# Other due times for the last element's normalisation pieces, squares and transpositions

## The reference

```
x = x + xattn(layernorm(x), ctx, ctx)
    # t = Wt v, p = Wp q, g = Wg k; att = sum over a group of p * g, 8 groups
    # y = Wz (att * t), group by group; group norm of y, times gn_w plus gn_b, plus v
x = x + ffn(layernorm(x))
    # t = x[:, perm] as 16 heads of 128; gelu(t up[h]) down[h]; back to the old order
```

## Time and profile before

| | us |
|---|---|
| median of 3 runs | 1515.17 (1512.41 to 1517.02) |
| profiled execution, its own time | 1520.61 |
| its span, first to last instruction | 1518.8 |
| PE busy | 1496.8 (99%) |
| DVE busy | 1201.1 (79%) |
| ACT busy | 1065.3 (70%) |
| POOL busy | 967.8 (64%) |

### The profile page before, as it was taken

The page is one execution under the profiler, slowest core; times in us unless marked ns, Lnnn a source line. Parts: engine busy times, 40 slices in busy tenths (PEclk is TensorE's granted clock), DMA queues, the critical chain, the costliest instruction groups (busy, mean ns, idle before and its releaser), DMA issues.

```text
span 1518.8 us, 19146 instructions
## 1 busy us (share of the span) xinstructions
PE 1496.8 (99%) x6592; PEld 1231.6 (81%) x6592; DVE 1201.1 (79%) x1514; ACT 1065.3 (70%) x1321; POOL 967.8 (64%) x765
## 2 busy tenths in 40 slices
PE   8999999999999999999999999999999999999998
PEld 7878887887878888888888888888888888877786
DVE  4999868887778767887778877887678876889786
ACT  4636757855778568784687847877478783899786
POOL 1673685298862668525794357835589264888787
PEclk9999999999999999999999999999999999999999
DMA  9998797786667937778376774767748676758886
GB/s 330 329 375 332 230 312 281 270 267 210 226 238 267 286 110 223 253 256 266 125 250 243 250 248 140 266 240 249 215 151 281 250 235 186 259 193 261 272 275 223
DMA packets 166865, 374.76 MB, mean 247 GB/s; under 512 B 14960, under 2 KB 80496, under 8 KB 158576
## 3 DMA queue, kind: packets, MB, share of 16 engines
q1 hardware_dynamic: 141424, 281.25, 56.3%
q0 software_dynamic: 25344, 92.29, 17.1%
HBM read 287.45 MB, written 86.03 MB: 246 GB/s over the span
## 4 chain that ended last, share of the span: by engine, by line
PE 69%; POOL 7%; DVE 7%; DMA 6%; ACT 5%; issue 4%; SPq 1%; POOLq 0%; ACTq 0%; DVEq 0%
PE PP L965 11%; PE PP L950 11%; PE PP L904 11%; PE PP L969 6%; PE PP L953 5%; PE PP L908 5%; PE PP L891 5%; PE PP L892 5%; PE PP L886 5%; PE PP L921 3%; PE PP L925 2%; DVE R L1096 2%; DMA WW<-w_scratch 1%; ACT Z L1043 1%; DMA FB<-xg_scratch,perm_sb 1%
## 5 line engine op out<-in xcount | busy, mean ns | idle before, releaser
L950 PE MATMUL PP<-GG,WW 128*128 128x512 f32 x1008 | 270.0, 390 | 1.0 <-DMA WW<-w_scratch 1.0
L1058 ACT ACTIVATE PP<-PP 128x1024 f32<-128x1024 f32 x256 | 262.1, 1024 | 0.0
L1261 DVE TENSOR_TENSOR R<-PP,R 128x1024 fp32r<-128x1024 f32 x175 | 213.6, 1220 | 55.0 <-ACT PP L1058 54.6
L904 PE MATMUL PP<-R,WC 128*128 128x512 f32 x1024 | 253.2, 389 | 0.2 <-ACT Z L1010 0.2
L1342 POOL TENSOR_TENSOR X<-X,RAW 128x512 f32<-128x512 f32 x112 | 192.5, 1753 | 95.3 <-DVE bn L1081 68.8
L1057 ACT ACTIVATE R<-PP 128x1024 fp32r<-128x1024 f32 x175 | 179.9, 1028 | 90.3 <-PE PP L953 90.0
L1096 DVE TENSOR_TENSOR R<-RAW,R 128x1024 fp32r<-128x1024 f32 x128 | 187.1, 1468 | 49.2 <-ACT R L988 49.2
L904 PEld LDWEIGHTS PP<-R,WC 128*128 128x128 f32 x1024 | 192.2, 188 | 40.6 <-ACT Z L1010 0.7
L950 PEld LDWEIGHTS PP<-GG,WW 128*128 128x128 f32 x1008 | 189.2, 188 | 41.3 <-issue 1.4
L1358 POOL DMA_INDIRECT out<-FB,perm_sb x128 | 150.7, 1177 | 83.0 <-DVE FB L1267 64.5
L891 PE MATMUL PP<-R 128*128 128x512 f32 x512 | 200.0, 391 | 0.2 <-DVE R L1096 0.2
(11 more groups left out here) (122 smaller groups left out, 2586.8 us busy)
## 6 DMA issues: line engine op xcount, KB each, us to landing
WW<-w_scratch SPq DMA_DIRECT2D x148, 512.0 KB, 5.2
X<-in_x SPq DMA_DIRECT2D x32, 1024.0 KB, 5.4
RAW<-in_cx SPq DMA_DIRECT2D x32, 1024.0 KB, 6.4
RAW<-in_xT SPq DMA_DIRECT2D x63, 512.0 KB, 5.7
RAW<-in_cT SPq DMA_DIRECT2D x63, 512.0 KB, 6.8
xg_scratch<-FB SPq DMA_DIRECT2D x104, 256.0 KB, 4.9
w_scratch<-WW POOLq DMA_DIRECT2D x16, 1024.0 KB, 6.8
HX<-wp_scratch SPq DMA_DIRECT2D x7, 1024.0 KB, 8.1
```

Of the source, the lines that this page charges most:

```text
L904: eng.matmul(PP[2 + ot // 2][:, ot % 2, :], WC[:, l, ct, part(ot)], u[:, ct, :], start=(l == 0 and ct == 0), stop=False)
L950: eng.matmul(pp[:, e, :], wt[:, l, part(2 * p + e)], g[:, 0, :], start=(l == 0), stop=False)
L1058: eng.activation(pp[:], pp[:], ACT.Gelu).then_inc(S["gelu"], 1)
L1261: eng.tensor_tensor(h_tile(f, p, 1), PP[slot["up", f, p]][:], f32(h_tile(f, p, 0)), ALU.subtract).then_inc(S["hlo"], 1)
```

## The change

In the last slot only, six kinds of due times are different. The pieces come at f0 + 5.3 + 2k instead of f0 + 7.25 + 2k, which puts each before the g_lo of a feed one earlier. The squares come 2.15 units after their piece instead of 1.2, which puts each behind the second gelu of a feed and ahead of the next g_hi, instead of between two gelus. The reference point e of the rest is f0 + 21.6 instead of f0 + 22.8; against it shift_x1 is 0.6 later, the second normalisations start at e + 1.9 with steps of 1.6 instead of e + 1.1 with 1.5, the transpositions are moved to e + 7.2, 9.8, 13.5 and 15.9, and each store comes 2.6 instead of 3 after its group's first transposition.

```diff
--- before.py
+++ after.py
@@ -657,29 +657,29 @@
         last = i == B - 1
         for k in range(8):
             ct, hf = k // 2, k % 2
-            t = f0 + 5 + 0.8 * k if first else f0 + 3.25 + 2 * (k + 2) if last else base[i + 1] - 0.3 + 0.95 * k
+            t = f0 + 5 + 0.8 * k if first else f0 + 5.3 + 2 * k if last else base[i + 1] - 0.3 + 0.95 * k
             put(t, x1_piece, i, ct, hf)
-            put(t + (1.2 if last else 0.9), square_x1, i, ct, hf)
+            put(t + (2.15 if last else 0.9), square_x1, i, ct, hf)
             if hf and not last:
                 put(t + 0.1, load_x, i + 1, ct)
         put(f0 + (4.1 if first else 5.26), mean_x1, i)
-        e = f0 + 12 if first else f0 + 22.8 if last else base[i + 1] + 8.6
+        e = f0 + 12 if first else f0 + 21.6 if last else base[i + 1] + 8.6
         put(e, sum_sq, i)
         put(e + 0.1, root_x1, i)
-        put(e + 0.9, shift_x1, i)
+        put(e + (1.5 if last else 0.9), shift_x1, i)
         put(e + 1.8, turn_sd, i)
         put(e + 1.9, store_sd, i)
         put(f0 + 43 if last else f0 + 29.5 if i == 0 else e + 5, spread_sd, i)
         for ct in range(NT):
             for half in range(2 if last else 0):
-                put(e + 1.1 + 1.5 * (4 * half + ct), xln2, i, ct, half)
+                put(e + 1.9 + 1.6 * (4 * half + ct), xln2, i, ct, half)
             if not last:
                 put(e + 1.1 + (0.6 if first else 0.9) * ct, xln2, i, ct)
         for q in range(NQ):
-            t = base[i + 1] + TURN[i][q] if not last else e + (6.2, 8.9, 12.1, 14.7)[q]
+            t = base[i + 1] + TURN[i][q] if not last else e + (7.2, 9.8, 13.5, 15.9)[q]
             for ct in range(NT):
                 put(t + (0.6 if last else 0.08 if (i, q) == (1, 3) else 0.25) * ct, turn, i, q, ct)
-            put(t + 3 if last else base[i + 1] + (32 if i == 1 else 28.3) if q == NQ - 1 else t + 1.3, store_x, i, q)
+            put(t + 2.6 if last else base[i + 1] + (32 if i == 1 else 28.3) if q == NQ - 1 else t + 1.3, store_x, i, q)
 
 
         ws = units(i)
```

## The result

| | before | changed |
|---|---|---|
| median of 22 runs, us | 1515.50 (1512.41 to 1517.60) | 1518.84 (1515.48 to 1522.50) |
| ratio, 95% interval | | 1.0019 (1.0012 to 1.0027) |
| profiled execution, us (span) | 1520.61 (1518.8) | 1519.32 (1517.5) |

A forecast was written before the change was run, and what follows sets the result against it. TensorE was taken as the bound, losing 0.5 us per feed to late g_lo. Gains of 2.0 (pieces) and 0.7 (root stage) less 0.2 (ScalarE order) gave 2.5 us: 1515.17 to 1512.7 us, range 1508.5 to 1517.8.

The forecast's parts named there:

- the two loops: While the eight pieces run, one by the squares (5.96 us) and one by GpSimd (5.93 us) hold VectorE's period.
- Loop S: Piece, its square, two GELUs on ScalarE, h_lo, next piece: 5.96 us per feed, with nothing waiting in it.
- Step 2: Squares after both GELUs: Loop S opens, a piece waits 0.65 us for the port; gain 2.0 us, bounds 0 and 2.0.
- Rival A: The port shared by VectorE and GpSimd binds at 5.93 us per feed; only 0.5 us gained, 1514.7 us; chance 0.20.
- The sign of being wrong: Wrong in sign if TensorE's five g_lo waits stay and a wait for weights is added.
- Step 1: Pieces one feed earlier, the first at 1304.9 us; cost put at 0, with 0.3 us of TensorE as bound.
- Step 3: sum_sq, root_x1, shift_x1 moved: 0.7 us gained (bounds 0 and 1.0), 0.2 given back for ScalarE's order.
- Step 4: Second normalisations and transpositions at new times: unchanged, bounds a loss of 1.0 and a gain of 0.9 us.
- Step 5: SyncE queue, store_x(7, 1) ahead of load_w(62, 0): load goes out 6.5 us later; cost 0, bound 1.8 us.
- rival C: Slower: load_w(62, 0) lands late behind the store, with the pieces' gain lost too; 1517.5 us; chance 0.12.
- Step 6: First feeds of element 7, gathers waiting for the fourth store: the whole gain of 2.5 us let through.

The follow-up runs named there:

- e6: Kernel before, with GpSimd's residual multiply and add for feeds 91 to 101 cut to 4 of 512 columns; ratio 0.9979.
- e10: Changed kernel with the squares back at 1.2 units behind their piece, pieces at their new earlier place; ratio 0.9985.
- e9: Changed kernel with each piece just behind the g_lo it stood ahead of, and store_x(7, 1) behind load_w(62, 0) again; 1511.66 us, ratio 0.9974.
- e7: Kernel before with only root_x1 moved ahead of the residual of feed 100 on GpSimd; ratio 0.9999.
- e12: Changed kernel with the squares back at 1.2 units behind their piece, and store_x(7, 1) behind load_w(62, 0) again; ratio 0.9979.
- e8: Changed kernel with each piece just behind the g_lo it stood ahead of; ratio 0.9982.

## Why the prediction was wrong

- **The bound and the measure** (first part) were right: PE's lost matmuls, the two loops, 0.5 us per feed. The statement that both loops last 5.95 us was not: Loop S alone is 5.55 us (e6, e10). It only looked as long because the piece in it carried 0.4 us of port wait. I had both numbers, 1.68 and 1.28 us for the piece, and subtracted them for DVE's work (4.76 us; 4.66 measured) but not here.
- **Step 2, the step that failed.** I priced the port with one wait per feed, of the piece, at its mean over all phases, 0.65 us, in 0.66 us of room. It costs 1.63 us: 0.53 for the piece and 1.10 for g_lo. The room was right: in e9 a wait of 0.77 us costs PE nothing. Two things were wrong. g_lo is a DVE operation of the same kind, with two operands in SBUF, and I didn't count it. And the phase isn't spread evenly: each engine's wait sets when it asks next, so they lock. In the changed kernel the DVE first ran ahead, 4.65 us from piece to piece, until a g_lo met POOL's add; from then on 6.30 (pieces and the third g_lo, order of time of DVE):

```profile
1302.04 1.28 DVE L1218 SCALAR_TENSOR_TENSOR Z<-Z,sm,X 128x1024 f32<-128x1024 f32 x1
...
1306.70 1.28 DVE L1218 SCALAR_TENSOR_TENSOR Z<-Z,sm,X 128x1024 f32<-128x1024 f32 x1
...
1311.35 1.28 DVE L1218 SCALAR_TENSOR_TENSOR Z<-Z,sm,X 128x1024 f32<-128x1024 f32 x1
1312.55 1.78 DVE L1256 TENSOR_TENSOR GG<-FB,GG 128x512 fp32r<-128x512 f32 x1
```

  Instead of gaining 2.0 us, the stretch up to unit 22 lost 2.0 more (3.6 against 1.6).
- **Rival A** named the mechanism, but priced it at 5.93 us, the period of the phase in the trace, and put it at no loss. That the same lock could be worse in another phase was in no case, so the range ended at 1517.8, 1.0 us below the result. Its argument that a piece which meets a gather costs neither side is not what e10 shows: a gather that starts while the piece runs takes 1.37 us instead of 0.97. The sign of being wrong that the prediction named, waits for g_lo that stay (four, 1.9 us) and a wait for weights added, is what came.
- **Step 1**: the first piece starts at 1302.04, in place of the forecast 1304.9 on the clock of before, which ran 2.75 us later; it is as forecast. With Loop S kept (e10) the pieces, started a feed earlier, run in the good phase; 0.9 us less are lost by unit 22 and, with the other new due times, 3.5 us less by unit 38. I had given the earlier start no gain of its own.
- **Step 3**: the root was to come sooner in the order, and did, but POOL was a feed behind: DVE waits 3.29 us, not less than 1.94. 1.9 us are lost at units 25 and 26 against 1.1. A due time is a place in a queue, and the queue of POOL is what decides. Where POOL isn't late (e10), the same due times give no wait at all. And in e7 a wait removed there is worth 0.1 us at unit 38: ACT and a port wait of g_lo take it back.
- **Step 4** (unchanged, -1.0 to +0.9): 1.1 us from unit 26 to 38 against 1.7 before; inside its bounds.
- **Step 5** and rival C's mechanism: 0.8 us of loss at feed 108, inside 0 to 1.8, where I took 0. The load went out when I said (1389.42; 1392.2 on the clock of before), but took 8.4 us to land, above the 4.2 to 7.7 of the earlier trace rows. In e10 it cost 1.85 us.
- **Step 6**: POOL waited 2.02 us instead of 4.67 for the fourth store, and ACT's wait for feed 113 ended at 1424.61 instead of 1424.84. From unit 40 to 52 the changed kernel loses 1.1 us, as the kernel before. As PE came no earlier, this kernel doesn't test whether the chain limits; the traces of e9 and e12, where PE did, lose 1.7 and 1.4 us there, and keep most of the gain.
- **The sum**: losses at unit 40 went up by 2.0 (pieces) - 0.3 (units 22 to 38) + 0.9 (weights) = 2.6 us; the time went up by 2.9.

## What to carry over

Where two engines block each other for the whole of an operation, list all operations of both that do so, with their order, and work out which phase the two queues settle in; a mean wait over all phases is no estimate. A wait that looks like pure loss may be what keeps an engine out of a worse phase: before it is removed, ask what the engine will run into when it comes earlier. A moved step is judged by how late its queue runs there, not by its due time.

## What the runs showed of the hardware

A DVE operation with two operands in SBUF (piece, g_lo) and a POOL multiply or add exclude each other, in both directions, for nearly their whole length: behind a piece the add took 2.17 us instead of 1.30 and ended 1.16 us after it, and behind an add the g_lo took 1.78 instead of 0.68 and ended 0.54 us after it. The DVE operations with one operand in PSUM (h_lo 1.21, add_r 0.67) kept their length beside both. A POOL scatter or gather that starts while a piece is well under way is longer (1.85 and 1.43 us instead of 1.02 and 0.97 in the changed kernel, at 1307.03 and 1302.73) and ends 0.90 and 0.84 us after the piece; a scatter that began 0.57 us before the piece is not (1.02, in e10). The same order of instructions held two stable periods, 5.95 and 5.55 us, and each came again in every trace of the kernels that have it (three, with the pieces where they were; two, with the pieces one feed earlier). The order of e8 and e9 gave one period, 5.43 us, in two phases: the g_lo took 0.70 us in one trace and 1.45 in the other.
